# Expert products of a mixture-of-experts layer in split halves, with the weights split by GpSimd in other stages

## The reference

```python
HIDDEN, NUM_EXPERTS, TOP_K, MOE_INTER, SHARED_INTER = 256, 8, 2, 176, 704

def _silu_and_mul(gu):
    i = gu.shape[-1] // 2
    return jax.nn.silu(gu[:, :i]) * gu[:, i:]

shared = _silu_and_mul(x @ shared_gate_up_w.T) @ shared_down_w.T
shared = shared * jax.nn.sigmoid(x @ shared_gate_w.T)
probs = jax.nn.softmax(x @ gate_w.T, axis=-1)
routing_weights, selected_experts = jax.lax.top_k(probs, TOP_K)
for e in range(NUM_EXPERTS):
    w_e = jnp.where(selected_experts == e, routing_weights, 0.0).sum(-1)
    h = _silu_and_mul(x @ w13[e].T) @ w2[e].T
    combined = combined + w_e[:, None] * h
out = shared + combined
```

## Time and profile before

| what | value |
|---|---|
| median of 3 runs | 1646.33 us (1643.37 to 1650.38) |
| profiled execution: span from first to last instruction | 1607.0 us |
| median minus that span | 39.3 us |
| mean granted TensorE clock | 0.995 |
| TensorE busy | 1491.0 us (93%) |
| VectorE (DVE) busy | 909.4 us (57%) |
| ScalarE (ACT) busy | 752.9 us (47%) |
| GpSimd (POOL) busy | 412.6 us (26%) |
| moved by DMA | 99.99 MB |

### The profile page before, as it was taken

The page is one execution under the profiler, slowest core; times in us unless marked ns, Lnnn a source line. Parts: engine busy times, 40 slices in busy tenths (PEclk is TensorE's granted clock), DMA queues, the critical chain, the costliest instruction groups (busy, mean ns, idle before and its releaser), DMA issues. The chain is left out here.

```text
span 1607.0 us, 28561 instructions
## 1 busy us (share of the span) xinstructions
PE 1491.0 (93%) x10462; PEld 1100.8 (68%) x10462; DVE 909.4 (57%) x1972; ACT 752.9 (47%) x1872; POOL 412.6 (26%) x328
## 2 busy tenths in 40 slices
PE   6999999998899899999999999998998998999898
PEld 4778877777677677778777767765555676533576
DVE  5766576666651656566565557147665515477712
ACT  5564656655334334343434433433443343677242
POOL 2706125040136142031211012622000461100173
PEclk9999999999999999999999999999999999999999
DMA  4103010010513421000010024221000523000533
GB/s 152 37 1 92 2 66 28 21 33 2 221 44 96 162 59 47 1 13 33 13 33 0 1 84 165 86 93 48 2 1 24 209 92 114 1 1 1 188 100 124
DMA packets 43143, 99.99 MB, mean 62 GB/s; under 512 B 7184, under 2 KB 21904, under 8 KB 42896
## 3 DMA queue, kind: packets, MB, share of 16 engines
q1 hardware_dynamic: 33040, 70.05, 12.9%
q0 software_dynamic: 9984, 28.32, 5.4%
HBM read 80.00 MB, written 18.35 MB: 61 GB/s over the span
## 5 line engine op out<-in xcount | busy, mean ns | idle before, releaser
L882 DVE TENSOR_TENSOR s_h_e<-s_bank,s_silu_e 128x176 f32<-128x176 f32 x92 | 31.2, 341 | 182.1 <-ACT s_silu_e L665 182.1
L527 PE MATMUL s_bank<-s_expert_w,s_xe 128*128 x368 | 124.8, 462 | 1.8 <-ACT s_xe L659 1.1
L384 POOL DMA_INDIRECT s_xg<-normed_rows,s_from_row x92 | 93.1, 1011 | 106.8 <-DVE s_from_row L790 79.9
L144 POOL TENSOR_SCALAR ln_var<-ln_moments 128x4 f32<-128x4 f32 x16 | 4.1, 255 | 450.7 <-DVE ln_moments L129 261.7
L391 POOL DMA_INDIRECT expert_rows<-s_y,s_to_row x92 | 91.1, 990 | 89.5 <-ACT s_y L677 71.5
L2645 POOL TENSOR_TENSOR s_w_hi<-s_w_raw,zero 128x1024 fp32r<-128x1024 f32 x25 | 55.6, 2222 | 211.0 <-PE s_memory L80 188.0
L1251 ACT ACTIVATE s_scratch<-s_bank,s_neg_max 128x128 f32<-128x128 f32 (+3 forms) x128 | 67.3, 528 | 84.9 <-DVE s_neg_max L1341 84.7
L551 PE MATMUL s_bank<-s_expert_w,s_he 88*128 x368 | 95.4, 381 | 4.9 <-ACT s_he L671 4.9
L1341 DVE TENSOR_REDUCE s_neg_max<-s_bank 128x1 f32<-128x128 f32 (+3 forms) x128 | 59.5, 487 | 55.9 <-PE s_bank L1141 55.7
L1139 PE MATMUL s_bank<-s_k,s_q 128*128 128x128 f32 (+3 forms) x256 | 88.6, 441 | 1.5 <-DVE s_v L1336 0.8
L551 PEld LDWEIGHTS s_bank<-s_expert_w,s_he 88*128 88x128 f32 x368 | 69.1, 189 | 29.7 <-issue 6.9
(11 more groups left out here) (398 smaller groups left out, 4291.0 us busy)
## 6 DMA issues: line engine op xcount, KB each, us to landing
s_expert_w<-in_experts SPq DMA_DIRECT2D x32, 608.0 KB, 13.5
s_w_raw<-in_wa_o SPq DMA_DIRECT2D x16, 512.0 KB, 3.5
s_yg<-expert_rows SPq DMA_DIRECT2D x32, 256.0 KB, 4.3
s_raw<-in_shared SPq DMA_DIRECT2D x16, 384.0 KB, 6.1
normed_rows<-s_ln_xn POOLq DMA_DIRECT2D x8, 512.0 KB, 9.5
s_w_raw<-in_wa_k SPq DMA_DIRECT2D x4, 512.0 KB, 3.8
s_w_raw<-in_wa_v SPq DMA_DIRECT2D x4, 512.0 KB, 3.5
s_w_raw<-in_wa_q SPq DMA_DIRECT2D x4, 512.0 KB, 4.3
```

The lines of the kernel that those rows point to most:

```text
L384: pool.indirect_dma_start(out=xg[:, i % XG_RING, :], out_offset=None, in_=x_rows[:, :], in_offset=bass.IndirectOffsetOnAxis(ap=from_row[:, ...
L527: last = pe.matmul(u_bank[i % 2][:, 0:2 * INTER], xe[:, i % 2, x], expert_of(P, i, w), start=c == 0, stop=c == DC - 1, skip_group_check=True)
```

## The change

The experts' products are made from halves like the others: x and h of each tile get a high part (ScalarE's copy, which now rounds) and a low part (a DVE subtraction, `low_x` and `low_h`), and both weights come as a high and a low tile. The halves of the weights aren't made in the mixture stages: a new helper `ExpertSplit` has GpSimd load a piece of an expert's weights, round it, subtract, and store both halves in DRAM, in the recurrent stage for the first mixture (16 pieces of 608 columns, four behind each group's splits) and in the wide stage for the second (8 pieces of 1216 columns, two ahead of the loop and two in each later group between the V and the O split; the hardware loop is unrolled for it). The mixture stages load both halves, sixteen transfers instead of eight, and wait for all of them ahead of the first tile. PE, ScalarE and DVE get another order in the tile loop. To make room, logits_t and yg share their place with tiles that are used at other times, and stages with two shared blocks hold two.

```diff
-        e = sb("expert_w", [P, N_EXP, EXP_COLS])
+        e_hi, e_lo = sb("expert_w_hi", [P, N_EXP, EXP_COLS], F32R), sb("expert_w_lo", [P, N_EXP, EXP_COLS], F32R)
...
                     for one in range(N_EXP):
-                        sp.dma_start(e[:, one, :], experts[one]).then_inc(e_loaded, 16)
+                        for to, part in zip((e_hi, e_lo), experts):
+                            sp.dma_start(f32(to[:, one, :]), part[one]).then_inc(e_loaded, 16)
...
             def expert_up(i):
-                pe.wait_ge(xe_done, i + 1)
+                pe.wait_ge(xe_lo_done, i + 1)
...
-                    last = pe.matmul(u_bank[i % 2][:, 0:2 * INTER], xe[:, i % 2, x], expert_of(P, i, w),
-                                     start=c == 0, stop=c == DC - 1, skip_group_check=True)
+                    last = product(pe, u_bank[i % 2][:, 0:2 * INTER], (xe_hi[:, i % 2, x], xe_lo[:, i % 2, x]),
+                                   expert_of(P, i, w), c == 0, c == DC - 1)
...
-                    last = pe.matmul(y_bank[i % 2][:, 0:D], he[0:IHALF, i % 2, h], expert_of(IHALF, i, w),
-                                     start=c == 0, stop=c == 1, skip_group_check=True)
+                    last = product(pe, y_bank[i % 2][:, 0:D], (he_hi[0:IHALF, i % 2, h], he_lo[0:IHALF, i % 2, h]),
+                                   expert_of(IHALF, i, w), c == 0, c == 1)
...
-            pe.wait_ge(e_loaded, 16 * N_EXP)
+            pe.wait_ge(e_loaded, 2 * 16 * N_EXP)
             find_owner(0)
             turn_x(0)
...
+            turn_x(3)
             turn_h(0)
+            find_owner(2)
+            expert_up(2)
             for i in range(TILES):
-                if i + 3 < TILES:
-                    turn_x(i + 3)
-                if i + 2 < TILES:
-                    find_owner(i + 2)
-                    expert_up(i + 2)
-                expert_down(i)
+                if i + 4 < TILES:
+                    turn_x(i + 4)
                 if i + 1 < TILES:
                     turn_h(i + 1)
+                expert_down(i)
+                if i + 3 < TILES:
+                    find_owner(i + 3)
+                    expert_up(i + 3)
...
+            def low_x(i):
+                dve.wait_ge(xe_hi_done, i + 1)
+                dve.tensor_tensor(xe_lo[:, i % 2, :], xt_bank[i % 2][:, 0:D], f32(xe_hi[:, i % 2, :]), ALU.subtract).then_inc(xe_lo_done, 1)
...
             for i in range(TILES):
-                h_of_tile(i)
+                if i + 2 < TILES:
+                    h_of_tile(i + 2)
+                if i + 4 < TILES:
+                    low_x(i + 4)
+                if i + 1 < TILES:
+                    low_h(i + 1)
...
-            with pool.Fori(1, GROUPS) as i:
-                split(i, (0, 1, 2))
+
+            if by_run:
+                for n in range(2):
+                    expert_split.piece(pool, n, n, 0, n == 0)
+            for i in range(1, GROUPS):
+                split(i, (0, 1))
+                if by_run:
+                    for n in range(2):
+                        expert_split.piece(pool, 2 * i + n, 2 * i + n, 0)
+                split(i, (2,))
                 move_q(i)
+            if by_run:
+                expert_split.end(pool, N_EXP)
...
-            groups(pool, group)
+            for G in range(GROUPS):
+                group(G, G < GROUPS - 1)
+                for n in range(4 * G, 4 * G + 4):
+                    expert_split.piece(pool, n, n // 2, n % 2 * E_PART, n == 0)
+            expert_split.end(pool, 2 * N_EXP)
...
+class ExpertSplit:
...
+    def piece(self, pool, n, expert, at, first=False):
+
+        cols = slice(at, at + self.columns)
+        of = lambda whole: whole[bass.ds(expert, 1), :, cols].rearrange("a p n -> (a p) n")
+        if not first:
+            pool.wait_ge(self.stored, 32 * n)
+        pool.dma_start(f32(self.lo[:]), of(self.experts)).then_inc(self.loaded, 16)
+        pool.wait_ge(self.loaded, 16 * n + 16)
+        pool.tensor_tensor(self.hi[:], f32(self.lo[:]), self.res.zero[:].broadcast_to([P, self.columns]), ALU.add).then_inc(self.hi_done, 1)
+        pool.wait_ge(self.hi_done, n + 1)
+        pool.tensor_tensor(self.lo[:], f32(self.lo[:]), f32(self.hi[:]), ALU.subtract).then_inc(self.lo_done, 1)
+        pool.dma_start(of(self.parts[0]), f32(self.hi[:])).then_inc(self.stored, 16)
+        pool.wait_ge(self.lo_done, n + 1)
+        pool.dma_start(of(self.parts[1]), f32(self.lo[:])).then_inc(self.stored, 16)
```

More of the change, by code:

```diff
@@ L36 @@
 XG_RING, Y_RING = 8, 8
+E_PART = EXP_COLS // 2
 AT_ORDER = P
@@ L256, in ffn_stage, with first_of @@
         sb = lambda what, shape, dt=F32: ctx.enter_context(nc.sbuf_tensor(f"{name}_{what}", shape, dt))
+        def first_of(what, shape):
+            with nc.sbuf_tensor(f"{name}_{what}", shape, F32) as first:
+                return first
         banks = [ctx.enter_context(nc.psum_tensor(f"{name}_bank{i}", [P, HALF], F32)) for i in range(8)]
@@ L883, in h_of_tile, with low_h @@
                                   ALU.mult).then_inc(h_e_done, 1)
+            def low_x(i):
+                dve.wait_ge(xe_hi_done, i + 1)
+                dve.tensor_tensor(xe_lo[:, i % 2, :], xt_bank[i % 2][:, 0:D], f32(xe_hi[:, i % 2, :]), ALU.subtract).then_inc(xe_lo_done, 1)
+            def low_h(i):
+                dve.wait_ge(he_hi_done, i + 1)
+                dve.tensor_tensor(he_lo[0:IHALF, i % 2, :], ht_bank[i % 2][0:IHALF, 0:D], f32(he_hi[0:IHALF, i % 2, :]),
+                                  ALU.subtract).then_inc(he_lo_done, 1)
+            low_x(0)
+            low_x(1)
             if early:
@@ L887, in _ @@
                     add_shared(b, 1)
-            for i in range(TILES):
-                h_of_tile(i)
+            h_of_tile(0)
+            low_x(2)
+            h_of_tile(1)
+            low_x(3)
+            low_h(0)
+            for i in range(TILES):
+                if i + 2 < TILES:
+                    h_of_tile(i + 2)
+                if i + 4 < TILES:
+                    low_x(i + 4)
+                if i + 1 < TILES:
+                    low_h(i + 1)
             for half in range(NHALF):
@@ L3147, in _, with __init__, end @@
             groups(dve, group)
+class ExpertSplit:
+    def __init__(self, nc, ctx, sem, name, res, experts, parts, columns):
+        sb = lambda what, dt: ctx.enter_context(nc.sbuf_tensor(f"{name}_{what}", [P, columns], dt))
+        self.res, self.experts, self.parts, self.columns = res, experts, parts, columns
+        self.hi, self.lo = sb("e_hi", F32R), sb("e_lo", F32R)
+        self.loaded, self.hi_done, self.lo_done, self.stored = (
+            sem("e_raw_loaded"), sem("e_hi_done"), sem("e_lo_done"), sem("e_stored"))
+    def piece(self, pool, n, expert, at, first=False):
[11 more added lines that the diff above has]
+        pool.dma_start(of(self.parts[1]), f32(self.lo[:])).then_inc(self.stored, 16)
+    def end(self, pool, n):
+        pool.wait_ge(self.stored, 32 * n)
 class Residual:
@@ L3207, in build_program @@
         t = {**t, "x_mid": nc.dram_tensor("x_mid", (SEG, SEGS // 2, 2, B, D), F32, kind="Internal").ap()}
+        for n in range(2):
+            t[f"experts{n}_parts"] = [nc.dram_tensor(f"experts{n}_{part}", (N_EXP, P, EXP_COLS), F32, kind="Internal").ap()
+                                      for part in ("hi", "lo")]
         rows = [nc.dram_tensor("normed_rows", (TOK, D), F32, kind="Internal").ap(),
@@ L3216, in build_program @@
             if kind == "L0_ffn":
[L3217 removed]
+                ffn_stage(nc, name, res, t["shared0"], t["experts0_parts"], t["gate0"], t["routing"], rows, True, False, "both" if n > 1 else "moments", None)
             if kind == "L0_attn_b":
@@ L3224, in build_program @@
             if kind == "L1_ffn":
-                ffn_stage(nc, name, res, t["shared1"], t["experts1"], t["gate1"], t["routing"], rows, False, True, "both" if n > 1 else "", out if n == len(stages) - 1 else None)
+                ffn_stage(nc, name, res, t["shared1"], t["experts1_parts"], t["gate1"], t["routing"], rows, False, True, "both" if n > 1 else "", out if n == len(stages) - 1 else None)
         nc.clear_and_free_semaphores(Semaphores.past.pop())
```

47 lines of the change are left out of this document (25 added, 22 removed).

## The result

The changed kernel takes 1681.49 us in the median (1677.36 to 1683.83) against 1646.07 before: ratio 1.0213, interval 1.0189 to 1.0237. It is 35 us slower; forecast were 1651.5 with a range of 1637 to 1667. To read the numbers the reader needs one thing more: the profiled execution of before that the prediction read was faster (span 1607.0) than every timed one, and a second profile of the same kernel, run here as the first experiment, has a span of 1647.6 at a time of 1649.3.

The account below looks back on a forecast made before the run. The prediction took TensorE, busy for nearly the whole span, as the bound, with GpSimd as slow in the tile loop. Its terms, -22 + 1 + 19.2 + 2 + 5 = +5.2, gave 1651.5 us, range 1637 to 1667.

Parts of the forecast that it names:

- The base: Whole kernel: span 1607.0 us, median 1646.33; the 39.3 us around the span taken as unchanged, the sum added to the median.
- The tile loop, -22: Four mixture stages: TensorE could go at 2.12 us a tile, GpSimd's 2.57 limits; -5.5 a stage, bounds -24 and -16.
- I take 48.0 from first to last scatter: Tile loop of each mixture stage: GpSimd alternates scatters and gathers at 2.57 us; 48.0 us where it was 53.5.
- Late start of stages 5 and 7, +19.2: Second half of expert weights delays the first turn by 9.6 us in each stage; bounds +10.4 and +22.
- the shorter head and the lower clock behind the wait: Stages 5 and 7: head from first turn to first scatter at most 2.2 us shorter, taken as equal to the lower clock's cost.
- Late shared blocks of stages 1 and 3, +1: Shared blocks queued on SP behind the doubled expert loads come later; +1 us for both stages together, bounds 0 and +4.
- covered by about 2 us in stage 1: First late shared block's up product at 454.26, its block ready by 452.0; less cover in stage 3.
- The splits, +2 and +5: GpSimd's added pieces slow DVE: +2 us in the recurrent stage (bounds 0, +5), +5 in the wide stage (0, +12).
- Rival (b): Recurrent and wide stages: GpSimd's operations hold DVE and the held time reaches PE; 26 us higher, 1677; chance 0.22.
- (c): Tile loop: register instructions add to each product, 2.67 us a tile, +5 a stage, about 1693 us; chance 0.05.
- (d): Tile loop: gathers keep up and tiles run at 2.12 us, 3 us a stage more gain, 1640 us; chance 0.08.
- (a): Stages 5 and 7 start late by the lower bound, +10.4, and the splits cost nothing: -11.6, 1634.7 us; chance 0.15.

Follow-up runs that it names:

- loop alone: Changed kernel with its tile loop only: no GpSimd splits in stages 0 and 2, expert weights loaded once and used for both parts; 1646.96 us, ratio 1.0000.
- the kernel with one load: Changed kernel with its splits and loop, but only the high parts of the expert weights loaded and used for both parts; 1656.0 us, ratio 1.0061.

## Why the prediction was wrong

**The base.** "some 39.3 us lie around the span; I take them as unchanged": this step failed first. In the second profile of before 1.7 us lie around the span, and 34.6 of the 40.6 us of difference stand inside the four tile loops. An unexplained 39 us between a span and the median was a sign that the profile was not of what is timed.

**The tile loop, -22: failed; 0 measured** (loop alone, 1.0000). The terms for TensorE and GpSimd were right: 2.11 us a tile where nothing is held, 2.57 us for a scatter and a gather. The step that failed is "I take 48.0 from first to last scatter": it lets GpSimd issue without a break and TensorE follow. Late signals break that, in both kernels: before's loops are 61 to 62.5 and the changed ones 59 to 61. Against the second profile of before the four loops of the loop alone are 5.4 us shorter in all, but their first scatters come 0.6, 0.1, 4.2 and 2.8 us later behind the stage's first load. So stages 5 and 7 even lose some 3 us each by the profiles, and stages 1 and 3 gain 1. That later first scatter of the new loop is a term that the sum hadn't.

**Late start of stages 5 and 7, +19.2: mechanism right, the size near it.** The loads run at the 424 GB/s that was taken; the 358 of the Trainium skill (“SBUF — State Buffer”, summary of rules for kernel authors) isn't what the windows show. The first turn is 10.8 and 11.6 us later than in the second profile of before, where 9.6 was forecast. The head from the first turn to the first scatter is 8.4 us in stage 5, and 11.6 with one load and the same order, so against the kernel with one load the first scatter is 7.6 and 8.8 later: 16.4. The forecast took the shorter head and the lower clock behind the wait as equal; here, clock included, the head is some 3 us shorter. That the sum came near is in part luck: the turns are later than forecast and the heads shorter.

**Late shared blocks of stages 1 and 3, +1: mis-sized.** The bounds were 0 and +4; against the kernel with one load the first turn is 2.0 us later in stage 1 and 7.1 in stage 3. The step that failed is "covered by about 2 us in stage 1": TensorE waits for the late block there too, 1.7 us. TensorE's waits in stage 3 (us, times, longest) and the windows:

```profile
PE s_bank L79 <- DVE s_w_lo L716: 3.6, 1, 3.6
```

```profile
1002.00:1008.00 6.00, 3.75 (x28) 3.36 (x27) 0.00 (x0) 0.58 (x1) 3.12 (x4) 1.00 1.02 404
1008.00:1014.00 6.00, 4.69 (x11) 3.74 (x12) 4.39 (x6) 3.74 (x7) 0.00 (x0) 0.52 0.04 13
```

The block is 3.6 us late in stage 3, with the DMA share full until 1008, and the granted clock then is at 0.52 (1.2 GHz) for six microseconds; with one load it stays at 1.00 there. So the wait comes with a slow stretch behind it, which would account for most of the other 3.5 of the 7.1 us; no run has the one without the other. The two late starts together are 25, where 20.2 stood.

**The splits, +2 and +5: nearly right.** 9 us measured between the two kernels with one load, without the splits and with them, and 2.0 and 6.6 by their profiles in stages 0 and 2. The normalisation went from a mean of 488 to 597 ns between these two (544 in the second profile of before, 612 in the changed kernel), so DVE is held, as forecast. TensorE's waits for s_q_next in stage 2, which DVE writes, without the splits and with them (us, times, longest):

```profile
PE s_bank L79 <- DVE s_q_next L1362: 2.2, 9, 0.4
...
PE s_bank L79 <- DVE s_q_next L1372: 8.4, 12, 1.6
```

All its waits for DVE there went from 5.3 to 11.9, the 6.6 by which the stage is longer, and in stage 0 from 30.3 to 32.0. Rival (b), which decides from 10 us of new waits on, stays below its mark with 8.3. The second profile of before is no good measure of this term: it has 6.1 us of waits for s_v in stage 2, where the changed kernel has 0.8, and in the profiles of kernels whose stage 2 isn't edited that stage takes from 400.3 to 404.7 us.

**The other rivals.** (c) falls: with its register instructions a tile takes 2.12 in the changed kernel without indirect transfers, as the first scatters there show (510.73 to 512.85). (d) and (a) needed the loop's gain. None of the rivals had the signals. With the measured terms the sum is 0 + 25 + 9 = 34 on the median of 1646: 1680, where 1681.5 was measured. Since the 25 was taken as the rest, this sum closes by its making; what bears it out are the 25.5 us of later starts by the profiles and the 32.6 without indirect transfers.

**What stays open.** Which part of the chip holds the signals, and why one execution was free of it. The faster execution of before ran the same indirect transfers at the same pace of 2.57 us without a late copy. So they are needed for the hold in these runs, as taking them out, or spacing them, ends it, but they aren't enough for it, and what else it takes no run shows. The records of the signals don't tell it either. Within the loops, of 92 for turns of x, 75 are recorded in the changed kernel and 78 in the second profile of before, and all 92 in the faster execution and with SP's transfers; but only 85 and 87 are in the two runs of the new loop without indirect transfers, where nothing is held. The Trainium skill, "NOTIFIC — the notification-queue block", section 7.1, says that the path that records travel can push back on the engine that makes them. That could hold an engine, but no run here was made without recording, so it isn't shown.

## What to carry to other kernels

Check first that span and time of a profile agree to a few microseconds; if they don't, as here, look for a second profile before trusting the first, since the difference can have its place in the stages. Before speeding up one engine in a loop, test what the loop gives with its neighbour's work taken out: here the same three products are worth 29.5 us without GpSimd's indirect transfers and nothing with them. Extra loads ahead of a stage's first product can cost more than the wait that they cause: 3.6 us of waiting in stage 3 went with a first turn 7.1 later, a part of it at the lower clock.

## What the runs showed that I had not expected

- In all but one of the profiles with back-to-back indirect transfers from GpSimd, TensorE's signals come late, by up to 2.5 us in the kernel before and 5.0 in the changed one, and in a long row its matmuls are held (0.7 us instead of 0.118). Direct transfers of the same bytes from SP don't do that: 0.9778. The Trainium skill, "DMA: Bandwidth & Descriptors", section "SWDGE vs HWDGE vs iDMA", says that GpSimd's cores write descriptors into rings in SBUF, and that SP's transfers don't touch that path; the run with SP's transfers agrees with that, but it changed the kind of transfer and the order of rows along with the issuer, and no run says anything on the rings.
- Spacing is enough: with a memset of 0.97 us between gathers, and a gather after every other scatter, the loop runs at 53.48 us instead of 61 to 62.
